# Second feed-forward projection on Trainium2: in the merged pass the hidden-activation loads are issued from POOL instead of SP, and the weight tiles get eight slots

## What is computed

```python
def _act_quant(a):
    scale = QB / jnp.clip(jnp.max(jnp.abs(a), axis=-1, keepdims=True), 1e-05)
    q = jnp.clip(jnp.round(a * scale), -QB, QB) / scale
...
h = _rmsnorm(x, norm_w)
gv = _bitlinear(h, w_gv)
value, gate = jnp.split(gv, 2, axis=-1)
h = value * jax.nn.silu(gate)
h = _bitlinear(h, w_out)        # (tokens, 8192) x (8192, 2048)
return residual + h
```

## Time and profile before

| | us |
|---|---|
| time before, median of 3 runs | 7273.61 |
| lowest and highest of them | 7215.04, 7617.41 |
| the profiled execution | 7242.26 |
| its span on the slowest core (core 4) | 7240.5 |
| spans of the eight cores | 7187.8 to 7240.5 |
| TensorE matmul busy | 4920.4 (68% of the span) |
| DVE, ACT, POOL busy | 2249.5, 1501.0, 366.7 |
| start of b = 0, first load | 6339.8 |
| start of b = 1, first load | 6510.3 |
| start of b = 2, first load | 6960.2 |

### The profile page before, as it was taken

The page is one execution under the profiler, slowest core; times in us unless marked ns, Lnnn a source line. Parts: engine busy times, 40 slices in busy tenths (PEclk is TensorE's granted clock), DMA queues, the critical chain, the costliest instruction groups (busy, mean ns, idle before and its releaser), DMA issues. The chain is left out here.

```text
span 7240.5 us, 63203 instructions; the slowest of 8 cores (7187.8 to 7240.5 us)
## 1 busy us (share of the span) xinstructions
PE 4920.4 (68%) x21575; PEld 2389.1 (33%) x21894; DVE 2249.5 (31%) x2790; ACT 1501.0 (21%) x2439; POOL 366.7 (5%) x620
## 2 busy tenths in 40 slices
PE   1666428998878876676776675388888873326677
PEld 1222113443433333332433432244344432212233
DVE  4100271000111113212222203655455536683310
ACT  4555520000000012101222200222222223321000
POOL 0111100000111100000000000000000000000000
PEclk9877658999998987787888887599999995558789
DMA  7899712111111111122111021433333319935556
GB/s 227 268 309 312 242 64 60 50 52 39 36 43 44 41 54 58 51 82 75 45 53 47 29 76 71 150 131 131 124 130 128 130 65 275 253 102 135 129 140 149
DMA packets 665414, 832.70 MB, mean 115 GB/s; under 512 B 434960, under 2 KB 518032, under 8 KB 608144
## 3 DMA queue, kind: packets, MB, share of 16 engines
q1 hardware_dynamic: 468368, 501.45, 23.0%
q0 software_dynamic: 49792, 268.47, 10.8%
q10 hardware_dynamic: 146944, 58.73, 3.0%
HBM read 702.66 MB, written 125.83 MB: 114 GB/s over the span
## 5 line engine op out<-in xcount | busy, mean ns | idle before, releaser
L1285 PE MATMUL PS_SC<-AF 128*128 128x512 bf16 x2048 | 802.4, 392 | 8.9 <-issue 1.8
L1279 PE MATMUL PS_SC<-AF 128*128 128x512 bf16 x1929 | 757.4, 393 | 60.4 <-PEq L1209 60.4
L653 PE MATMUL PS_D<-AF 128*128 128x512 bf16 x2257 | 532.0, 395 | 149.0 <-ACT AF L673 146.0
L904 PE MATMUL PS_C<-AF 128*128 128x512 f32 (+3 forms) x768 | 405.5, 618 | 324.7 <-ACT AF L984 322.2
L653 PE MATMUL PS_C<-AF 128*128 128x512 bf16 x2258 | 532.3, 395 | 90.7 <-ACT AF L673 64.8
L1648 PE MATMUL PS_SC<-AF 128*128 128x512 bf16 x2002 | 505.3, 410 | 65.0 <-DVE AF L1614 32.7
L748 PE MATMUL PS_C<-AF 128*128 128x512 bf16 x1506 | 343.6, 386 | 150.4 <-DVE AF L723 148.8
L179 ACT ACTIVATE AF<-AF 128x2048 f32<-128x2048 f32 x192 | 366.3, 1909 | 276.2 <-DMA AF<-wgv 184.0
L653 PEld LDWEIGHTS PS_D<-AF 128*128 128x128 bf16 x2304 | 231.5, 101 | 444.2 <-issue 193.8
L871 PE MATMUL PS_SC<-AF 128*128 128x512 f32 (+1 forms) x640 | 316.6, 632 | 70.5 <-DMA AF<-Qscr 47.9
L616 DVE CAST AF<-AF 128x2048 bf16<-128x2048 f32 x32 | 39.3, 1229 | 1042.2 <-PE PS_D L653 1012.5
(11 more groups left out here) (160 smaller groups left out, 5575.5 us busy)
## 6 DMA issues: line engine op xcount, KB each, us to landing
AF<-wgv POOLq DMA_DIRECT2D x128, 1024.0 KB, 8.8
AF<-wgv SPq DMA_DIRECT2D x128, 1024.0 KB, 4.9
AF<-wout POOLq DMA_DIRECT2D x64, 1024.0 KB, 7.4
AF<-wout SPq DMA_DIRECT2D x64, 1024.0 KB, 7.6
AF<-TOUT SPq DMA_DIRECT2D x512, 128.0 KB, 2.9
AF<-wo SPq DMA_DIRECT2D x128, 256.0 KB, 6.1
HMID<-AF POOLq DMA_DIRECT2D x128, 256.0 KB, 2.8
TOUT<-AF ACTq DMA_DIRECT2D x128, 256.0 KB, 6.1
```

The source lines that it names most:

```text
L653: _pe_last = te.matmul(ps, self.bap(2 * wb[h % 2] + c * 128, [[1, 128]]), self.bap(2 * xb + c * ncols + grp * 512, [[1, 512]]), start=(c = ...
L904: te.matmul(self.PS_C.ap()[:, qlo * 128:512], self.af(VB0 + (h % 3) * 2048 + kt * 128, 128), self.af(PTB0 + (kt % 2) * 512 + qlo * 128, 51 ...
L1279: te.matmul(psv, self.bap(2 * AQ1T + c * 1024 + qt * 128, [[1, 128]]), self.bap(2 * (TT0 + mp * 8192) + c * 512, [[1, 512]]), start=(c == ...
L1285: _l = te.matmul(psg, self.bap(2 * AQ1T + c * 1024 + qt * 128, [[1, 128]]), self.bap(2 * (TT0 + mp * 8192 + 4096) + c * 512, [[1, 512]]), ...
```

## The change

In the merged pass the HMID loads go from SP's list to POOL's. They use three buffers and the semaphores G0, G1 and GP, so that L0 to L3 become free and the weight tiles have eight slots in both multiplying passes. Load k on POOL waits for the rounding of block k-3. POOL's list for quarter j is now: the y stores of quarter j-1, the 16 HMID loads of quarter j; the stores of quarter 3 come last. SP's list in the merged pass becomes that of the last pass. b = 0 and b = 2 stay as they are.

```diff
-            TS_Q = TSEM if b == 1 else TSEM + ["L0", "L1", "L2", "L3"]
+            TS_Q = TSEM + ["L0", "L1", "L2", "L3"]
...
-                    if bld and mm:
-                        for j in range(4):
-                            for kk in range(16):
-                                hm2_load(j * 16 + kk)
-                                for o4 in range(4):
-                                    tob_load(j, 4 * kk + o4)
-                            for qt in range(4):
-                                x1_load(j, qt)
-                    elif bld:
+                    if bld and not mm:
                         for k in range(64):
                             hm2_load(k)
                     else:
...
                             def pre(k=k):
-                                lp = f"L{k % 4}"
-                                v.wait_ge(self.sems[lp], c0[lp] + 16 * (k // 4 + 1))
+                                if mm:
+                                    q = ["G0", "G1", "GP"][k % 3]
+                                    v.wait_ge(self.sems[q],
+                                              c0[q] + 16 * (k // 3 + 1))
+                                else:
+                                    lp = f"L{k % 4}"
+                                    v.wait_ge(self.sems[lp],
+                                              c0[lp] + 16 * (k // 4 + 1))
                                 if k >= 2:
                                     v.wait_ge(self.sems["PE"], PEn[("T", k - 2)])
-                            hm = self.af(HM2 + (k % 4) * 512, 512)
+                            hm = self.af(HM2 + (k % (3 if mm else 4)) * 512, 512)
...
                     def _(gp):
-                        for j in range(4):
+                        def ystores(j):
                             for qt in range(4):
...
+                        for j in range(4):
+                            if j >= 1:
+                                ystores(j - 1)
+                            if bld:
+                                for kk in range(16):
+                                    k = j * 16 + kk
+                                    if k >= 3:
+                                        gp.wait_ge(self.sems["DV"],
+                                                   DVn[("rnd", k - 3)])
+                                    i = b * 4 + j
+                                    self.dma(gp,
+                                             self.af(HM2 + (k % 3) * 512, 512),
+                                             self.HMID.ap()[i * 128:(i + 1) * 128,
+                                                            kk * 512:(kk + 1) * 512],
+                                             ["G0", "G1", "GP"][k % 3])
+                        ystores(3)
```

## The result

| | before | after |
|---|---|---|
| median of the runs | 7377.61 us (10 runs) | 7245.26 us (9 runs) |
| lowest | 7215.04 | 7112.26 |
| the profiled execution | 7242.26 | 7136.93 |
| span of its slowest core | 7240.5 (core 4) | 7135.1 (core 5) |
| ratio, 95% interval | | 0.9834 (0.9788 to 0.988) |

In many executions of both kernels the cores of one die are granted a lower clock and take longer; the medians hold these, the ratio leaves them out, and the experiments are read on cores of the other die. The ratio says 1.7% faster, with an interval that reaches from 1.2% to 2.1%, so that these runs don't settle whether the gain is over 2%.

The account below looks back on a forecast made before the run. The prediction took the SP load-order ring to bound the merged pass. Its terms, -136.1 + 3 + 7.2 + 0.5 = -125.4 us, took 7242.3 to 7116.9, stated as 7117, range 7080 to 7180.

Parts of the forecast that it names:

- The ring on SP: Merged pass: next HMID load waits on SP behind weight loads awaiting TensorE's slots; loosening it saves 136.1 us over four quarters.
- where the runs fall, which lie 0.4% to either side: Whole-kernel time: run spread of 0.4% either way, deciding whether the gain reads over 2%; 30 us added at each range end.
- I charge 3 us for tiles that come late all the same: Inside the merged pass's quarters: late weight tiles still cost +3 us, between 0 and 10.8.
- 10.9 + 0.4 + 0.5 + 3.0 + 2.9 = 17.7 us: Merged-pass quarter end: fourth y operation, store start, store issue, HMID landing, rounding; bounds 17.3 to 20.6, three ends +7.2.
- The start of the pass: +0.5: Start of the merged pass: POOL's first HMID load replaces SP's, costing +0.5 us.
- 86.6: Merged pass: TensorE's waits for L202 without those at quarter ends, 132.5 - 45.9 us, one of three parts of the gain.
- The first (DMA side too tight): Merged-pass quarters: DMA is tighter than its mean share, a block taking 4.4 us instead of 3.86; +34, 7151 us; chance 0.12.
- the second (POOL's load late): Merged pass: POOL's HMID loads land late, deciding from 8.7 us; at 12 us, +70, 7187 us; chance 0.06.
- The fourth: Merged pass: POOL's queue becomes the ring; at 17.2 us landings, +45 and +7 at the ends, 7294 us; chance 0.03.
- The third: Merged pass: only SP's issue time is bought, 64 issues or 29 us, as the ring persists elsewhere; 7213 us; chance 0.05.
- (1) and (2): Merged-pass quarters: HMID loads move to POOL, and SP keeps weight and X1 loads with eight weight slots; together -136.1 us.
- The rule against it: POOL's HMID loads: VectorE locks GpSimd out of the descriptor port, making a load 2.5 us later, inside the slack, same sum.

## Why the prediction was right and wrong

**The mechanism was right.** The ring on SP, its price and what is late next came out as reckoned: quarters of 61.8 us were forecast and 61.2 to 61.9 measured on the profiled core, -136.1 us against -136.5; the clock is at 0.95 or more; DVE's wait for HMID gave way to one for the transposes. The DMA share is 0.75 to 0.81 for the 0.78 worked out from the earlier trace rows. The ratio says -1.7%, which is what 7117 is to the profiled execution of before.

**The stated range failed.** The median of the nine runs, 7245, lies above the 7180 at which the range ended. The step that failed is "where the runs fall, which lie 0.4% to either side", and the 30 us that the range was given for it at each end: it took its spread from two of the three runs in the table and passed over the third, 7617.41, which is 5.6% above the lowest. What the runs showed in its place is a spread of that size: the nine of the changed kernel go from 7112 to 7514 us, five of them from 7245 up, and the ten of the kernel before from 7215 to 7659. The four fastest runs of the changed kernel, 7112 to 7137, lie inside the range, to either side of 7117.

**Terms that were mis-sized**, in the order of the sum:

- *"I charge 3 us for tiles that come late all the same"*: nothing of it was measured. Tiles land in a median of 4.1 us where 2.9 was taken, and 6.3 were there.
- *"10.9 + 0.4 + 0.5 + 3.0 + 2.9 = 17.7 us"* for an end: 18.3 to 21.3 on the eight cores, mean 19.6, and 20.6 on the slowest. The failing number is the 3.0 for a landing. Over the 24 ends of the eight cores the parts are 10.6 us to the end of the fourth y operation, 1.1 from there to the issue of the load, 5.0 until DVE starts on it, and 2.9 for the rounding. So the three ends cost +15.8 on the slowest core where +7.2 was forecast, at the edge of its bounds of +6.0 to +15.9. (On core 5 a wait for a y store grew besides, to 5.89 us in the end shown, for what had been 5.06 in the last pass of the kernel before, on core 4; in the mean the y side is as reckoned.) Which of the transfers crowds which is settled only in part. With four weight slots in place of eight the 5.0 is 4.3, with the weights held back it is 6.1, and with two HMID loads at once instead of three it is 5.1 (means of cores 4 to 7).
- *"The start of the pass: +0.5"*: +2.1. From the first load of the pass to the first transpose it takes 7.1 to 8.4 us on the eight cores, for 5.5 to 5.8 before. With HMID on SP, where the first load goes alone ahead of the weights, it is 5.5 to 6.1; with four weight slots on POOL it is still 7.0 to 7.7 (cores 4 to 7), so that eight weight loads in place of four don't explain it. What does was not tried apart.
- *"Passes 0 and 2 and all that is ahead of them keep their orders"* is so, but the stretch between the merged and the last pass grew by 3.7 us, which the sum left out (see the last section).
- *"86.6"* us of waits for L202 inside the quarters holds 7.8 too many: the 128.8 of the earlier trace rows begin with TensorE's wait ahead of the first transposes, which is no part of a quarter. Inside them it is 78.9 us, with 10.8 for weights, and TensorE's busy time fell from 290.5 to 246.6 us in the four, 43.8, for the "38.7 that remain". The sum doesn't use this split.
- Nothing could foresee the +11.7 of the stages ahead; it lies within the spread of the same stages in the other executions.

By its terms the pass was to save 125.4 us and saved 118.6 up to its last matmul. That the time came out at 7136.9 and not 7117 is these 7 us, the 3.7 and the 11.7, less 2.

**The rivals.** The first (DMA side too tight) and the second (POOL's load late) fell: the loads landed late, but inside the slack, as the runs with two buffers and with doubled loads show from the other side. The fourth needed landings of 15 us, and the longest HMID landing on any core was 7.4. The third fell as well. Its mechanism, a ring that persists, is refuted by the four waits left for L202, and the queue by itself, with four slots, brought 51.6 us where the rival had 29 for the issue time. Only once the ring is loosened is a further queue worth little: with eight slots, HMID on SP comes within 6 us of HMID on POOL. The rule named beside this rival, of the Trainium skill, "Trainium Kernel Development and Optimization", section "Key Constraints", counts the sequencer's time alone. The 51.6 us are more than that; they are the wait of one load that no longer holds up another behind it. The prediction treated (1) and (2) as one edit and never asked what each is worth alone.

**The rule against it.** The trace of the kernel before shows what the 821 ns of the earlier trace rows are. Core 4, DVE and POOL in the stage that stores HMID:

```profile
4676.32 1.29 DVE L1240 TENSOR_SCALAR AF<-AF,V_sgv 128x2048 bf16<-128x2048 f32 x1 [0.30 <-issue]
4676.58 1.15 POOL L147 DMA_DIRECT2D HMID<-AF  x1 [215.50 <-DVE RMX L1263]
...
5952.43 0.54 POOL L147 DMA_DIRECT2D HMID<-AF  x1 [6.37 <-DVE RMX L1263]
```

105 of the 128 issues begin while DVE is in a TENSOR_SCALAR of L1240, and every one of them ends 116 to 128 ns after that instruction ends; the first one shown does so at 4677.73, for 4677.61. The other 23 begin beside an idle DVE and take 539 to 542 ns. The Trainium skill, "SBUF — State Buffer", section "SBUF: two separate sides", would have POOL's descriptors wait for DVE. The trace agrees. In the merged and the last pass the same thing is rare and short: of the 768 issues that POOL makes there on the eight cores of the changed kernel, 8 take 562 to 767 ns, and each of them ends 118 to 120 ns after a TENSOR_SCALAR of DVE's. The 64 HMID issues of a core have a median of 536 to 538 ns, since most of them begin when a rounding has just ended, and DVE's operations take 0.4 to 0.7 us each there. So the wait exists, and in this pass it costs nothing that can be seen; loads from ACT land as late as those from POOL.

## What to carry to other kernels

When a load is late because its queue is blocked by another load's wait, ask first how deep that other load's buffering is: here more slots did nearly all of it, and a second queue on top, with its loads behind the stores, gave back at the ends of the quarters most of what it gained inside them. When a load moves to another queue, look at what stands ahead of it there, and put loads that need nothing ahead of stores that wait; with buffers enough and the next work rounded in advance, an end went from 19.5 to 5.9 us. Once an engine is fully busy in a stage, the stage's ends are where time is left.

## What was not expected of the hardware

At the end of a block every engine has a DRAIN, and the next block waits for it. POOL's is much longer if POOL issued the HMID loads of the pass. Instructions of the line that ends the block, duration ns min/median/max; the kernel before, then the changed one:

```profile
L1512 POOLq DRAIN  x1: 3606/3606/3606, 6955.0 to 6955.0; - x1
```

```profile
L1512 POOLq DRAIN  x1: 7162/7162/7162, 6847.8 to 6847.8; - x1
```

7162 to 7164 ns stood there in all seven kernels that issue the 64 loads on POOL once, whatever their ends looked like, and 3.2 to 4.1 us in the kernel before and with HMID on SP or ACT, where POOL issued the stores of y alone. With the 128 loads of the doubled run it was 4.2 to 4.4 us, so it is no simple count of what was issued; what sets it stays open. It fits the 3.7 us between the passes: the mean of that stretch on cores 4 to 7 is 17.6 us before, 20.8 after, and 18.1 and 18.2 with HMID on SP and on ACT. With four y buffers the DRAIN begins 6.1 us after the last matmul, for 9.3 to 10.9 in the changed kernel, and is as long as ever, and the stretch is 18.1 us: there, too, the next block begins when it is over.
